# Graph kernel: one-column products in place of written zeros, and edge products grouped by type

## What is computed

```python
def step(h, _):
    messages = h[col] @ W_msg.T + b_msg
    agg = jax.ops.segment_sum(messages, row, num_segments=num_nodes)
    ...
def _gnn_layer(edge_index, x, edge_attr, norm, We, be, Wn, bn):
    parts = [x[src], x[dst]] + ([edge_attr] if edge_attr is not None else [])
    e = relu(concatenate(parts, axis=-1) @ We + be)
    agg = segment_sum(e * norm[:, None], dst, num_segments=x.shape[0])
    return relu(concatenate([x, agg], axis=-1) @ Wn + bn), e
x = layernorm(x + gru(x));  x = layernorm(x + three_layers(x))
```

## Time and profile before

| | us |
|---|---|
| median of 3 runs (2203.95 to 2209.13) | 2204.12 |
| the profiled execution | 2204.84 |
| its span, first to last instruction | 2202.6 |
| TensorE busy (86%) | 1899.2 |
| VectorE busy (64%) | 1403.0 |
| GpSimd busy (46%) | 1006.2 |
| ScalarE busy (29%) | 647.0 |

### The profile page before, as it was taken

How to read it: one execution, slowest core, us unless ns; L and a number is a source line. 1 busy time by engine, 2 the same in 40 slices (tenths; PEclk the granted TensorE clock), 3 DMA queues, 4 the chain that set the end, 5 groups by cost and what they waited for, 6 DMA issues and landing times. The chain is left out here.

```text
span 2202.6 us, 47924 instructions
## 1 busy us (share of the span) xinstructions
PE 1899.2 (86%) x14264; PEld 1461.4 (66%) x14264; DVE 1403.0 (64%) x4662; ACT 647.0 (29%) x1271; POOL 1006.2 (46%) x1015
## 2 busy tenths in 40 slices
PE   6777669999999995588888877999999969999994
PEld 3433234545454543488888756999999859899993
DVE  6999741313132324588888854777777548788885
ACT  0168841212121211333333331333333322121111
POOL 0588700000000000377777725666666257777770
PEclk9688879999999997899999997999999989999998
DMA  3036770000000003445555525777777445555551
GB/s 99 14 78 108 108 64 0 0 0 0 0 0 0 0 0 126 163 149 151 155 155 149 148 90 151 216 217 215 217 216 217 127 116 157 142 158 146 157 150 36
DMA packets 193648, 242.12 MB, mean 110 GB/s; under 512 B 56276, under 2 KB 120047, under 8 KB 192799
## 3 DMA queue, kind: packets, MB, share of 16 engines
q1 hardware_dynamic: 161023, 172.73, 27.9%
q0 software_dynamic: 31840, 57.21, 11.1%
q10 hardware_dynamic: 576, 9.44, 1.1%
HBM read 149.75 MB, written 69.88 MB: 100 GB/s over the span
## 5 line engine op out<-in xcount | busy, mean ns | idle before, releaser
L1523 POOL DMA_INDIRECT rows<-p_dram,src_i x864 | 829.9, 961 | 348.0 <-issue 239.1
L1755 DVE TENSOR_TENSOR agg_t<-psum,agg_t 128x128 f32 x1380 | 393.3, 285 | 186.4 <-PE psum L1634 165.1
L1614 PE MATMUL psum<-w_c,before 128*128 128x128 f32 x1840 | 410.1, 305 | 0.0
L902 PE MATMUL psum<-adj,parts 128*128 (+2 forms) x1750 | 339.9, 352 | 5.3 <-ACT agg L981 4.4
L1603 PE MATMUL psum<-p_sb,pair_src 128*128 x1032 | 229.1, 306 | 108.2 <-DVE pair_dst L1729 65.4
L1688 ACT ACTIVATE rows<-rows 128x512 f32<-128x512 f32 x216 | 136.1, 630 | 578.8 <-DVE rows L1748 575.0
L1739 DVE TENSOR_SCALAR hot_w<-col_f,dst_loc,weight 128x128 f32<-128x128 f32 x864 | 302.7, 354 | 0.5
L1614 PEld LDWEIGHTS psum<-w_c,before 128*128 128x128 f32 x1840 | 282.4, 194 | 0.0
L902 PEld LDWEIGHTS psum<-adj,parts 128*128 128x128 f16 x1750 | 153.1, 98 | 190.9 <-issue 23.7
L1275 POOL MEMSET agg_t<- 128x3200 f32 x1 | 2.8, 2765 | 604.0 <-POOLq L1038 604.0
L1610 PE MATMUL psum<-q_parts,hot_all 128*128 x2592 | 252.3, 220 | 0.0
(11 more groups left out here) (242 smaller groups left out, 2455.5 us busy)
## 6 DMA issues: line engine op xcount, KB each, us to landing
e_dram<-after SPq DMA_DIRECT2D x230, 256.0 KB
before<-e_dram SPq DMA_DIRECT2D x230, 256.0 KB
adj<-stage SPq DMA_DIRECT2D x196, 97.8 KB
pair_rows<-sorted_rows SPq DMA_DIRECT2D x129, 128.0 KB
rows<-p_dram,src_i POOLq DMA_INDIRECT x864
hot_all<-dst_rows ACTq DMA_DIRECT2D x2, 3072.0 KB, 15.0
p_dram<-p_sb SPq DMA_DIRECT2D x6, 384.0 KB
records<-record_of,place_i POOLq DMA_INDIRECT x128
```

The costliest lines, as they stand in the source:

```text
L902: mm = nc.tensor.matmul(psum[:, AGG_BANK, 0:n_cols], parts[:, w, part, :], adj[:, w, cols], start=(w == 0 and part == 0), stop=(w == WINDO ...
L1523: nc.gpsimd.indirect_dma_start(out=rows[:, b % ROWS, m * D:(m + 1) * D], out_offset=None, in_=p_dram, in_offset=bass.IndirectOffsetOnAxis( ...
L1614: mm = nc.tensor.matmul(o, before[:, q % BEFORE, m * P:(m + 1) * P], w_c[:], start=False, stop=True)
L1755: nc.vector.tensor_tensor(a, psum[:, A_BANKS[q % len(A_BANKS)], m * P:(m + 1) * P], a, ALU.add).then_inc(agg_on, 1)
```

## The change

In the adjacency ScalarE writes no zeros, and the table of zeros and its semaphore go. TensorE starts each step with a product of one column (`begin`, line 661 of the changed kernel) into column 511 of the *next* band's bank with `start=True`. It uses the same target marks as weights; its value is not read. `start=True` makes the bank take the next band's first product in place of what it holds. A bank may be begun anew once ScalarE has copied it, so TensorE now waits for the copies (`staged`, which begins at 7).

In the edge passes the products of a quad go in three loops: the float32 products of a sorted quad for all four tiles, then the twelve bfloat16 products, then the four float32 products with `w_c`; only a bank's first product has `start=True`.

```diff
         @block.tensor
         def _(pe):
+            def begin(bank, hot, s):
+
+                nc.tensor.matmul(psum[:, bank, CHUNK - 1:CHUNK], hot, src_hot[:, s % MOVES, 0:1],
+                                 start=True, stop=False, skip_group_check=True)
+
             for s in range(BAND_STEPS):
...
                 bank = nc.s_assert_within(nth & (BANKS - 1), 0, BANKS - 1,
                                           skip_runtime_bounds_check_because="three bits of the band's number")
+                following = nc.s_assert_within((nth + 1) & (BANKS - 1), 0, BANKS - 1,
+                                               skip_runtime_bounds_check_because="three bits of the next band's")
...
-                    pe.wait_ge(free, values[last % PE_AT_ONCE] & 255)
-                nc.tensor.matmul(psum[:, bass.ds(bank, 1), 0:SPAN],
-                                 dst_hot[:, s // HOT_BATCH % BATCHES, s % HOT_BATCH // SIDE, :, s % SIDE],
+                    pe.wait_ge(staged, values[last % PE_AT_ONCE] & 255)
+                hot = dst_hot[:, s // HOT_BATCH % BATCHES, s % HOT_BATCH // SIDE, :, s % SIDE]
+                if s == 0:
+                    begin(slice(1, 2), hot, s)
+                begin(bass.ds(following, 1), hot, s)
+                nc.tensor.matmul(psum[:, bass.ds(bank, 1), 0:SPAN], hot,
                                  src_hot[:, s % MOVES, 0:SPAN], start=False, stop=False,
                                  skip_group_check=True).then_inc(counted, 1)
...
             nc.scalar.preload_act_table(ACT.Copy)
-            act.wait_ge(zeroed, 1)
-            for b in range(BANKS):
-                nc.scalar.copy(psum[:, (b + 1) % BANKS, 0:SPAN], zeros[:]).then_inc(free, 1)
+            act.sem_inc(staged, BANKS - 1)
             for g in range(BANDS):
...
                 nc.scalar.copy(stage[:, g % STAGES, :], psum[:, (g + 1) % BANKS, 0:SPAN]).then_inc(staged, 1)
-                if 1 <= g <= BANDS - BANKS:
-                    act.wait_ge(staged, g)
-                    nc.scalar.copy(psum[:, g % BANKS, 0:SPAN], zeros[:]).then_inc(free, 1)
...
+                def sums(m):
+                    return psum[:, E_BANKS[q % len(E_BANKS)], m * D:(m + 1) * D]
+
+                if i is not None:
+                    for m in range(QUAD):
+                        nc.tensor.matmul(sums(m), pair_src[:, i % PAIRS, m, :],
+                                         t["p_sb"][:, bass.ds(values[m], 1), :],
+                                         start=(m == 0), stop=False, skip_group_check=True)
                 for m in range(QUAD):
-                    o = psum[:, E_BANKS[q % len(E_BANKS)], m * D:(m + 1) * D]
                     if i is not None:
-                        nc.tensor.matmul(o, pair_src[:, i % PAIRS, m, :], t["p_sb"][:, bass.ds(values[m], 1), :],
-                                         start=True, stop=False)
...
                     for part in range(3):
-                        mm = nc.tensor.matmul(o, hot, t["q_parts"][:, bass.ds(window, 1), part, :],
-                                              start=(part == 0 and i is None),
-                                              stop=(part == 2 and e_before is None))
-                    if e_before is not None:
-                        mm = nc.tensor.matmul(o, before[:, q % BEFORE, m * P:(m + 1) * P], w_c[:],
-                                              start=False, stop=True)
+                        mm = nc.tensor.matmul(sums(m), hot, t["q_parts"][:, bass.ds(window, 1), part, :],
+                                              start=(i is None and m == 0 and part == 0),
+                                              stop=(part == 2 and e_before is None), skip_group_check=True)
+                if e_before is not None:
+                    for m in range(QUAD):
+                        mm = nc.tensor.matmul(sums(m), before[:, q % BEFORE, m * P:(m + 1) * P], w_c[:],
+                                              start=False, stop=True, skip_group_check=True)
```

More of the change, by code:

```diff
@@ L614, in build_adjacency @@
         stage = sb("stage", [P, STAGES, SPAN], F16)
-        zeros = sb("zeros", [P, SPAN], F16)
         zeroed = sem("zeroed")
@@ L621, in build_adjacency @@
         counted = sem("counted_a")
-        free = sem("bank_free")
         staged = sem("staged")
@@ L629, in _ @@
         def _(pool):
-            nc.gpsimd.memset(zeros[:], 0.0).then_inc(zeroed, 1)
-            pool.wait_ge(zeroed, 1)
             last = (BANDS - 1) % SPANS * BAND + BAND
@@ L709, in _ @@
                 a = g % SPANS * BAND
-                sp.wait_ge(staged, g + 1)
+                sp.wait_ge(staged, BANKS + g)
                 sp.dma_start(adj[a:a + BAND, g // SPANS, :].rearrange("d (a b) -> d a b", a=SPANS),
@@ L714, in _ @@
                 sp.wait_ge(laid[i], 16 * len(range(i, BANDS, STAGES)))
-            sp.wait_ge(zeroed, 2)
+            sp.wait_ge(zeroed, 1)
             sp.wait_ge(keep["placed"], 16 * SORT_STEPS)
```

## The result

The changed kernel takes **2367.49 us** (median of 4 runs, 2361.85 to 2374.89) against 2204.73 (2203.95 to 2209.13) of the kernel before: a ratio of 1.0736, 95% interval 1.0702 to 1.077, slower by 163 us. Forecast were 2341 us, with 2312 to 2366 as range; the result lies 1.5 us above it. The direction and the place were right, and so was the mechanism of the largest term, but its size was too small.

A forecast was written before the change was run, and what follows sets the result against it. TensorE's sequencer was taken to bound the adjacency, TensorE the second edge pass, the gathers passes one and three. 2204.84 + 160 - 3 - 20 = 2341.8; with the median 0.7 lower, about 2341 us, range 2312 to 2366.

The forecast's parts named there:

- The sequencer of TensorE is the bound of the adjacency, 90% full: Adjacency: TensorE's instruction stream alone needs 196 us of the 216.5 us from first to last product.
- 0.31 us a step for the addition, 182 us: Adjacency: each added one-column product, with two register operations and an address operation, costs 0.31 us, 182 over 586 steps.
- The start at 77.5: Adjacency: the first product comes at about 77.5 us instead of 79.02, as TensorE need not wait for zeros.
- -3 us behind the last product: Adjacency's end: copies and stores no longer queue, one of each remains; -3 us, between 0 and -9.
- -20 us from the edges: Edge passes: fewer changes between float32 and bfloat16 save 16 us in pass two, 3 in three, 1 in one.
- The array's time is what counts: Rival, adjacency: the added sequencer operations pass while VectorE is waited for; 2174 us, chance 0.06.
- register operations come cheap: Rival, adjacency: only the address operation with its product is paid, 0.12 us a step, 70 us; total 2229 us, chance 0.07.
- no gain at the edges: Rival, edge passes: twelve bfloat16 products starve on the sequencer, the saving comes back as waits; 2361 us, chance 0.10.
- the clock: Rival, adjacency: at the lower clock a step has 0.63 us of array time, half the steps pay 0.06 more; 2359 us, chance 0.07.

The follow-up runs named there:

- e3_two_ops: The kernel before with two more register operations ahead of each wide product of the adjacency, no product more: 2302.01 us, ratio 1.0437.
- e5_half_columns: The changed kernel with the adjacency's wide product on 195 of 391 columns, banks cleared once by VectorE: 2365.07 us, ratio 1.072 to the kernel before.
- e2_adjacency: The kernel before with the adjacency part of the change alone, edge passes as before: 2383.65 us, ratio 1.081.
- e1_edges: The kernel before with the edge part of the change alone, adjacency as before: 2192.87 us, ratio 0.9937.
- e7_product: The kernel before with a one-column product and its address operation ahead of each wide one, no register operation more, ScalarE's zeros kept: 2268.25 us, ratio 1.0282.

## Why the prediction was right or wrong

- **The sequencer of TensorE is the bound of the adjacency, 90% full.** Right. Two register operations without any product cost 97.8 us (e3_two_ops), and half the array work saved nothing (e5_half_columns).
- **0.31 us a step for the addition, 182 us.** This is the step that failed, by its size. The stage took 396.6 us; less 20 table loads of 2.08 that is 0.606 a step, against (196 - 44) / 586 = 0.259 before: 0.347 us, or 203 us in all. I had priced the address operation and its product by line 1610 (0.12, read from starts given to a tenth) and the register operations by the mask's (0.09 to 0.10). The added ones are each longer: 36 ns of a row instead of 32, and 60 instead of 46. From a wide product's load to the next small one's pass 0.33 us in three of four steps inside a group, about 0.02 more than I had. In the other steps the sequencer stalls for some hundredths more. By the starts in the trace such stalls come after every 20 to 22 of TensorE's instructions, whichever stands there (a weight load and its product counted as two): 265 in the stage, some 12 us together or 0.02 a step, and as many in e5_half_columns. That is enough for the rest of the missing 0.037. What the sequencer stalls for, the profile doesn't show, and it was not tried. My spread of 0.30 to 0.33 had no room for stalls at all, and of two readings, 0.31 and 0.32, I took the lower.
- **The start at 77.5.** Right in number (77.2 for the first one-column product), but by luck. In the profiled execution the stage opened 2.4 us earlier, behind parts that the change doesn't touch, as ScalarE's first instruction in it shows, before and after:

```profile
74.56 1.28 ACT L688 ACT_TABLE_LOAD   x1 [74.56 <-PEq L165]
72.14 1.28 ACT L694 ACT_TABLE_LOAD   x1 [72.14 <-PEq L165]
```

From there to the first product passed 5.0 us, in e2_adjacency too; before it was 4.5. The wait for the zeros went, but the one for the marks took its place (9.0 us idle), because VectorE's copy ahead of the marks lasted 2.8 us instead of 0.5.

- **-3 us behind the last product.** It was -4.7.
- **-20 us from the edges.** Pass two gave 13.6 to 14.1 us by its gathers, where I had 16; passes one and three give nothing that repeats. That changes of type cost TensorE time is shown by the order that removes them and by the one that adds them. But I had the wrong change: nothing is lost at the return from float32 to bfloat16. The first float32 pass behind a bfloat16 product takes 0.165 us to the next instead of 0.112 (the pair of 0.28 in a mixed tile). The sum came out all the same by luck, because in both orders a quad has as many changes of the one kind as of the other: 460 of them in the pass became 115, 18 us of TensorE's time by the trace.
- **The rivals.** "The array's time is what counts" falls with e5_half_columns, "register operations come cheap" with e3_two_ops, "no gain at the edges" with e1_edges. Of "the clock" the condition came true, the lower level for the whole stage, and its 2359 us lie nearer to the result. But its mechanism is not what happened: steps inside a group came 0.55 to 0.58 us apart (201.31, 201.89, 202.44, 203.01), closer than its 0.63, and half the columns changed nothing. The floor of small matmuls in the Trainium skill ("TensorE: Matmul & The Clock Gate", part 1) does not set the price here: 62.6 us for 586 products in e7_product are 0.107 each, and 0.14 with the 20 us of slack that they used up, where that floor would make 0.025.

## What to carry to other kernels

A product whose address comes from a register had a price on the sequencer here that no busy time shows (62.6 us for 586 in e7_product): look at "idle before, issue" on the weight loads and at the spacing of bare products before adding one, however few its columns. Where a stage's engines are all near full (here TensorE's sequencer 196, VectorE 206 of 216 us), moving work to one of them can be paid at the receiver's price in full, as it was here. And take apart a change of two parts: here the part that saves 12 us was hidden under the one that costs 179.

## What the runs showed that I had not expected

The granted clock. From 79 to 295 us it was 0.84 of full speed in the kernel before and 0.50, the lower of the two levels (1.2 GHz) without a break, in the changed one and in e3_two_ops; e7_product, which puts the same products closer together, had 0.79. The same window (columns as in the earlier trace rows) of the changed kernel,

```profile
79.00:295.00 216.00, 178.77 (x640) 66.43 (x640) 132.81 (x363) 36.85 (x76) 76.20 (x80) 0.50 0.15 37
```

of e3_two_ops,

```profile
79.00:295.00 216.00, 178.00 (x402) 41.80 (x402) 155.31 (x463) 94.90 (x220) 98.44 (x101) 0.50 0.22 52
```

and of e7_product:

```profile
79.00:295.00 216.00, 175.47 (x902) 90.96 (x903) 168.63 (x517) 111.63 (x262) 109.61 (x113) 0.79 0.27 62
```

In the changed kernel the longer products at the lower clock cost nothing that can be seen, since half the columns saved nothing in e5_half_columns at the same 0.50; no run has that kernel's sequencer work at the upper level. A busy share of 178 in 216 us there is long products at the lower clock, not a full engine.
